# A fused cross-attention kernel: the opening reordered, with the image-prompt V and U products moved into the loop

## The chip, the core and the metric

The kernel runs on one core of one Trainium2 chip. The metric is the time of one execution on the device, in microseconds (us), the median of several runs. Its matmuls are in 32-bit floats, or in pairs of fp32r parts (a high part and the remainder) where precision allows.

## The reference, cut to what matters

Eight batches of 512 tokens (320 channels, 20 heads of 16) attend to 60 text tokens and 4 image-prompt (ip) tokens of a context of width 512.

```python
q = heads(x @ W_q)
k_t, v_t = heads(text @ W_k), heads(text @ W_v)
probs_t  = softmax(q @ k_t.T * D**-0.5)
text_out = probs_t @ v_t
k_ip, v_ip = heads(ip @ W_k_ip), heads(ip @ W_v_ip)
qsem = l2norm(probs_t @ text)
sem  = qsem @ l2norm(ip).T
probs_ip = softmax(q @ k_ip.T * D**-0.5 + 0.5 * sem) * spatial_mask
out = (text_out + probs_ip @ v_ip) @ W_out + b_out + x
```

## The kernel before, in words

The program is written for five engines by hand: each block of the source (`sync`, `gpsimd`, `scalar`, `vector`, `tensor`) is the order of one engine's queue, and semaphores tie them together. Nothing reorders it.

**The loop.** The work is cut into 160 units: 32 tiles of 128 tokens, and 5 groups of 4 heads in each. Twenty units make a batch, ten make a half of 256 tokens. In its slot `u` TensorE (L1230 to L1260) transposes the exps of unit `u + 2`, makes the scores of unit `u + 4`, does at most one task of the table `MISC`, and multiplies unit `u`'s transposed exps with a table (L1062, `table_products`); the table holds the Gram matrix of the context, three differences of ip tokens and V, so that one product gives the weighted sums and what the l2 norm needs. `table_products(u)` waits until ScalarE has copied unit `u - 2` out of the same bank (`copy_fin`). ScalarE's slot `u` (L689) holds in this order: `copy_fin(u - 2)`, a copy of the previous task's bank, the exps of unit `u + 3`, the copy of unit `u + 2`'s transposed exps, and in some slots a few more. VectorE's slot `u` (L886) has the maxima of unit `u + 3`, the end of the previous task, and the quadratic forms of unit `u - 1`.

`MISC` (L278 to L292) gives units their tasks: `q` projects the next half's queries in three parts, `x` transposes the half after that, `at` and `o` (from unit 19 on) transpose a tile's attention and project it to the output. These tasks use the two banks of `mi_ps` in turn, in the order of `MISC_ORDER`; `bank_released` (L311) names the semaphore on which a task waits for its bank, that of two tasks before.

**U.** The ip part of the output is folded into a product: U is W_out applied to the ip differences of V, one row per head and difference. Five U products go to `u_sb`; SP then places batch by batch the rows that belong to it into `u_nat` by small transfers (`place_u`, L355), and once for all batches the last 64 rows of W_out and the bias as broadcasts (`u_shared`, L366, L367). SP waits for all five copies (L364). ScalarE splits a batch's rows into a high part at the end of the slot that `u_batch` names (L716 to L720: unit 12 of each batch) after a wait for `u_shared` and `u_placed`; VectorE makes the low part one slot later (L925).

**The opening** is all that stands before slot 0, and its order is that of the source. SP loads the context in four pairs of batches (the ip tokens once more behind the first pair, L336), x's first half, then W_v, W_k, W_k_ip, W_q (three transfers), W_v_ip, W_out, the mask and more of x. TensorE transposes the context by pairs (L1136), the scaled ip tokens (L1141) and x's first half (L1009, L1011). The transposed context is kept twice: `ctxT`, and `ctxM`, whose ip columns are replaced by differences of the scaled ip tokens (L815 to L820). Gram is `ctxT` times `ctxM` (L1150). ScalarE casts the whole `ctxT` to its high part in one instruction (L653), VectorE subtracts for the low part (L824); the same is done for the weights. V is three products for each pair, high by high, low by high, high by low (L1156): three pairs now, the last one later (L1207). Three K products (L1176) alternate with the first half's three query parts; ScalarE (L667) and VectorE (L843) split K, and POOL (`km_step`, L418) spreads it over heads. Then come the scores of units 0 and 1, the ip V product (`vip`, L1201), V's last pair, x's second half, and, with the scores of units 2 and 3 among them, the five U products (L1216), whose copies ScalarE makes (L682).

Of the kernel before, what the change touches and what calls it, by code (L numbers as in the profile page):

```python
# [35 lines left out]
P = 128  # L36
# [8 lines left out]
def xattn_kernel(nc, x, ctx_tokens, ip_mask, w_q, w_k, w_v, w_k_ip, w_v_ip, w_out, b_out, out):  # L45
# [35 lines left out]
    with es:  # L81
# [17 lines left out]
        def again(place, *shape):  # L99
# [25 lines left out]
        ctxT, ctxM = (  # L125
            place_ctxT[:, EC * B * TOK * n:EC * B * TOK * (n + 1)].rearrange("p (c t) -> p c t", c=EC) for n in range(2))
# [71 lines left out]
        ctxT_act, ctxT_dve, ctxM_text, ctxM_made = (  # L198
            sem("ctxT_act"), sem("ctxT_dve"), sem("ctxM_text"), sem("ctxM_made"))
# [121 lines left out]
        K_BANKS, U_BANKS = (5, 4, 3), (3, 4, 5, 3, 4)  # L321

        def u_batch(u):

            b, s = divmod(u, UNITS)
            return b if s == 12 and b < B else None
# [5 lines left out]
        def _(sp):  # L332
            for q in range(PAIRS):
                sp.dma_start(ctx_nat[:, q, :], ctx_tokens.rearrange("(q b) t e -> q (b t) e", b=2)[q]).then_inc(in_ctx[q], DMA)
                if q == 0:
                    sp.dma_start(ip_nat[:], ctx_tokens[:, T:TOK, :]).then_inc(in_ip, DMA)  # L336
# [3 lines left out]
            sp.dma_start(wkip, w_k_ip.rearrange("(c p) n -> p c n", p=P)).then_inc(in_wkip, DMA)  # L340

# [6 lines left out]
            load_square(wq_nat, w_q, in_wq, (0, 64))  # L348
            sp.dma_start(wvip, w_v_ip.rearrange("(c p) n -> p c n", p=P)).then_inc(in_wvip, DMA)
# [32 lines left out]
        def _(pool):  # L382
# [79 lines left out]
            def builds(t, part):  # L462
# [5 lines left out]
                if k == 0 and b == 0:  # L468
                    pool.wait_ge(v_copied, PAIRS)
# [110 lines left out]
        def _(act):  # L580

            nc.scalar.preload_act_table_set("natural_log_exp_and_others")
# [69 lines left out]
            act.wait_ge(ctxT_dve, 2)  # L652
            nc.scalar.copy(ctx_hi, ctxT).then_inc(ctx_hi_made, 1)  # L653
# [6 lines left out]
            act.wait_ge(in_wo, 2 * DMA)  # L660
            nc.scalar.copy(wo_parts[:, 0], wo[:, 0:2]).then_inc(wo_hi_made, 1)
# [4 lines left out]
            for m in range(QC):  # L666
# [5 lines left out]
                if m > 0:  # L672
                    q_high(0, m - 1)
            q_high(0, 2)
            exps(0)
            exps(1)
            act.wait_ge(pre_v, PAIRS)
# [73 lines left out]
        def _(dve):  # L751
# [55 lines left out]
            for q in (1, 3):  # L807
                dve.wait_ge(pre_ctxT, q + 1)
                v.tensor_copy(ctxT[:, :, P * q:P * q + P], BANKS[q].rearrange("p (c t) -> p c t", c=EC)).then_inc(ctxT_dve, 1)
                if q == 1:  # L810
                    dve.wait_ge(ip_rn_made, 1)
                    v.tensor_scalar(ipn[:], ip_nat[:], ip_rn[:], SEM_SCALE, ALU.mult, ALU.mult).then_inc(ipn_made, 1)

            dve.wait_ge(pre_ipn, 1)
            ip_cols = ctxM.rearrange("p c (b t) -> p (c b) t", t=TOK)  # L815
# [16 lines left out]
            for r in range(2):  # L832
# [3 lines left out]
            by_batch = ctxT.rearrange("p c (b t) -> p c b t", t=TOK)  # L836
            v.tensor_tensor(ip_dif[:, :, :, 0:NDIF], by_batch[:, :, :, T:T + NDIF],
                            by_batch[:, :, :, TOK - 1:TOK].to_broadcast([P, EC, B, NDIF]), ALU.subtract)
            v.tensor_copy(ip_dif[:, :, :, NDIF:NIP], by_batch[:, :, :, TOK - 1:TOK]).then_inc(ip_dif_made, 1)
            dve.wait_ge(wo_hi_made, 1)  # L840
            v.tensor_tensor(wo_parts[:, 1], wo[:, 0:2], wo_parts[:, 0].bitcast(F32), ALU.subtract).then_inc(wo_lo_made, 1)
            for m in range(QC):
# [8 lines left out]
                if m == 1:  # L851
                    q_low(0, 0)
            maxima(0)
            q_low(0, 1)
            maxima(1)
            q_low(0, 2)

            dve.wait_ge(pre_vip, 1)
# [136 lines left out]
        def _(pe):  # L995
# [173 lines left out]
            for q in range(PAIRS - 1):  # L1169
                v_product(q, BANKS[q])  # L1170
# [119 lines left out]
```

## Time and profile before

| | us |
|---|---|
| median of 3 runs (lowest, highest) | 322.41 (321.0, 322.69) |
| the profiled execution | 320.57 |
| its span, first to last instruction | 318.9 |
| start of slot 0 in it | 44.83 |

In that execution PE (TensorE) was busy for 95% of the span, ScalarE (ACT) for 87%, VectorE (DVE) for 84%, GpSimd (POOL) for 66%. The mean granted clock of TensorE was 1.000.

A row of the timeline gives the start, the length, the engine, the line of the source, the operation with its output and inputs, the sizes and how many instructions are merged; in brackets is how long the engine stood idle before and what released it. PEld is TensorE's weight load. Matmuls are pipelined: a merged row ends with the end of its last product, which is later than the start of the next row. A chain of waits is followed back from the last instruction; its pieces are what the end waited for, one after the other.

### The profile page before, as it was taken

Reading aid. Unit: us, or ns where it says so; the run is one execution under the profiler, and the core shown is the slowest. Engines: PE = TensorE matmul, PEld = TensorE weight load, DVE = VectorE, ACT = ScalarE, POOL = GpSimd, SP = SyncE. Lnnn points to the kernel's source line nnn. Section 1 sums busy time; section 2 is a strip of 40 time slices with the busy share of each in tenths; the row PEclk is TensorE's granted clock in tenths of the full one; section 3 lists DMA queues with packets and bytes.
Section 4 is the critical chain, followed back from the end, with each engine's and each line's share of the span. In section 5 each row is a group of like instructions: output and inputs, shape, how many; then the busy total and the mean of one; then the engine's idle time right before and its main releaser. Section 6 shows DMA issues by size and latency. Waiting matters only on the chain.

```text
span 318.9 us, 8813 instructions
## 1 busy us (share of the span) xinstructions
PE 302.9 (95%) x2289; PEld 288.6 (91%) x2289; DVE 268.1 (84%) x1861; ACT 276.3 (87%) x1168; POOL 210.4 (66%) x372
## 2 busy tenths in 40 slices
PE   4899899999999999999999999999999999998976
PEld 3798769888999999999999999999999999998964
DVE  5766847898889888988898889897998899888985
ACT  3736589999999999999999999989999999999942
POOL 3043328688878687878968786778787878676200
PEclk9999999999999999999999999999999999999999
DMA  6980003000120212011201111011202120010011
GB/s 206 346 238 0 1 13 85 2 2 2 32 64 25 62 32 64 24 63 32 63 25 39 47 30 53 15 62 36 62 24 63 34 62 24 23 33 22 23 43 64
DMA packets 15130, 17.02 MB, mean 53 GB/s; under 512 B 2592, under 2 KB 14536, under 8 KB 15080
## 3 DMA queue, kind: packets, MB, share of 16 engines
q1 hardware_dynamic: 15080, 16.44, 16.8%
q8 instruction: 20, 0.33, 0.5%
q14 instruction: 30, 0.25, 0.3%
HBM read 10.55 MB, written 5.24 MB: 50 GB/s over the span
## 4 chain that ended last, share of the span: by engine, by line
PE 70%; DVE 14%; ACT 11%; issue 1%; DMA 1%; POOL 1%; SPq 1%; POOLq 0%
PE gv_ps L1072 19%; PE mi_ps L1107 12%; PE mi_ps L1031 11%; PE et_ps L1059 9%; PE sc_ps L1051 8%; ACT e_sb L619 7%; DVE place_ctxT L795 4%; DVE xl L759 2%; DVE negmax L787 2%; PE mi_ps L1085 2%; PE gv_ps L1186 2%; PE mi_ps L1009 2%; DMA place_ctx<-in_ctx 1%; DVE ktok L847 1%; PE sc_ps L1166 1%
## 5 line engine op out<-in xcount | busy, mean ns | idle before, releaser
L619 ACT ACTIVATE e_sb<-sc_ps,negmax 128x60 f32<-128x60 f32 x640 | 152.0, 349 | 4.9 <-DVE negmax L787 2.9
L795 DVE CUSTOM_DVE_ANT_0 place_ctxT<-gv_ps,e_sb 128x60 f32<-128x60 f32 x640 | 101.0, 213 | 21.9 <-PE gv_ps L1072 19.7
L1072 PE MATMUL gv_ps<-tab,place_w 128*128 128x160 f32 x640 | 113.2, 299 | 0.0
L1072 PEld LDWEIGHTS gv_ps<-tab,place_w 128*128 128x128 f32 x640 | 93.7, 189 | 0.3 <-ACT place_w L637 0.2
L1051 PE MATMUL sc_ps<-km,qs 128*128 128x256 f32 x320 | 77.0, 322 | 0.1
L637 ACT COPY place_w<-et_ps 128x256 f32<-128x256 f32 x160 | 67.0, 419 | 0.2
L1059 PE MATMUL et_ps<-ident,e_sb 128*128 128x128 f32 x320 | 62.6, 277 | 4.4 <-ACT e_sb L619 1.9
L787 DVE TENSOR_REDUCE negmax<-sc_ps 128x4 f32<-128x240 f32 x160 | 63.5, 397 | 0.0
L795 DVE DVE_READ_ACCUMULATOR2_ANT quad<- 128x1 f32 x640 | 52.6, 82 | 0.0
L1059 PEld LDWEIGHTS et_ps<-ident,e_sb 128*128 128x128 f32 x320 | 41.5, 141 | 11.0 <-ACT e_sb L619 9.8
L420 POOL TENSOR_TENSOR km<-ktok,group_mask 128x512 fp32r<-128x512 f32 x40 | 41.3, 1040 | 14.3 <-DVE ktok L847 7.8
L628 ACT COPY fin<-gv_ps 128x80 f32<-128x80 f32 x160 | 43.1, 269 | 6.8 <-DVE quad L795 5.7
L1051 PEld LDWEIGHTS sc_ps<-km,qs 128*128 128x128 f32 x320 | 48.3, 191 | 0.5 <-issue 0.3
L496 POOL TENSOR_TENSOR qs<-q_full,qs 64x256 fp32r<-64x256 f32 x60 | 43.8, 730 | 4.8
L494 POOL CAST qs<-q_full 64x256 fp32r<-64x256 f32 x60 | 23.6, 393 | 27.7 <-ACT q_full L597 25.7
L516 POOL TENSOR_TENSOR mixed<-fin,place_ctxT 128x640 f32<-128x640 f32 (+1 forms) x18 | 21.6, 1202 | 15.7 <-DVE place_ctxT L942 9.7
L786 DVE COPY sip<-sc_ps 128x12 f32<-128x12 f32 x160 | 26.0, 163 | 3.3 <-PE sc_ps L1051 3.1
L1107 PE MATMUL mi_ps<-wo_parts,attnT 128*128 128x320 f32 x120 | 22.8, 311 | 0.0
L884 DVE TENSOR_TENSOR place_w<-mi_ps,x_nat 128x320 f32<-128x320 f32 x31 | 14.9, 484 | 5.3 <-PE mi_ps L1107 5.3
L433 POOL COPY tab<-g_sb 60x315 f32<-60x315 f32 x32 | 14.8, 461 | 6.5 <-POOL tab L433 3.1
L1107 PE MATMUL mi_ps<-wo_parts,attnT_low 128*128 128x320 f32 x60 | 19.0, 323 | 0.0
L1031 PE MATMUL mi_ps<-xl,wq_hi 128*128 128x256 f32 (+1 forms) x96 | 19.0, 279 | 0.0
(184 smaller groups left out, 550.6 us busy)
## 6 DMA issues: line engine op xcount, KB each, us to landing
x_nat<-in_x SPq DMA_DIRECT2D x16, 320.0 KB, 3.1
out<-place_w SPq DMA_DIRECT2D x32, 160.0 KB, 1.8
place_ctx<-in_ctx SPq DMA_DIRECT2D x4, 256.0 KB, 3.1
place_w<-in_L_xattn_W_v SPq DMA_DIRECT2D x1, 640.0 KB, 6.3
place_w<-in_L_xattn_W_k SPq DMA_DIRECT2D x1, 640.0 KB, 7.6
place_w<-in_L_xattn_W_k_ip SPq DMA_DIRECT2D x1, 640.0 KB, 9.0
place_w<-in_L_xattn_W_v_ip SPq DMA_DIRECT2D x1, 640.0 KB, 9.1
place_ctxT<-in_L_xattn_W_out SPq DMA_DIRECT2D x1, 640.0 KB
```

What stands on the lines that cost most here:

```text
L420: g.tensor_tensor(km[:, b % 2, c].rearrange("p s (j t) -> p s j t", t=TOK), ktok[:, :, c, TOK * b:TOK * b + TOK].unsqueeze(2).to_broadcast ...
L496: g.tensor_tensor(qs[other, half % 2, c, :], q_full[own, m, :], qs[own, half % 2, c, :].bitcast(F32), ALU.subtract).then_inc(q_part, 1)
L619: last = nc.scalar.activation(e_sb[:, slot, TOK * j:TOK * j + T], sc_ps[:, bank, TOK * j:TOK * j + T], ACT.Exp, bias=negmax[:, slot, j:j + 1])
L628: nc.scalar.copy(fin[:, t % TILES, GROUP * c:GROUP * c + GROUP, :], ps[:, :, T:TABW]).then_inc(fin_copied, 1)
L637: nc.scalar.copy(eT[:, u % TRING, :], et_ps[:, u % 2, 0:2 * P]).then_inc(eT_copied, 1)
L787: v.tensor_reduce(negmax[:, u % ERING, :], ps[:, :, 0:T], AX_X, ALU.max, negate=True).then_inc(max_done, 1)
L795: last = v.tensor_tensor_reduce(out=junk[:, u % 2, j, 0:T], in0=gv_ps[:, u % 2, TABW * j:TABW * j + T], in1=e_sb[:, u % ERING, TOK * j:TOK ...
L1031: last = mm(to, w, xx, start=n == 0, stop=n == len(steps) - 1)
L1051: last = mm(sc_ps[:, u % 2, 0:GROUP * TOK], q, km[:, parity, c, part, :], start=part == 0, stop=part == 1)
L1059: last = tr(et_ps[:, u % 2, P * r:P * r + P], e_sb[:, u % ERING, P * r:P * r + P], ident[:])
L1072: last = mm(gv_ps[:, u % 2, 2 * TABW * r:2 * TABW * r + 2 * TABW], eT[:, u % TRING, P * r:P * r + P], tab[:, b % 2, h:h + 2, :].rearrange( ...
L1107: last = mm(ps, steps[n][0], steps[n][1], start=n == 0, stop=n == len(steps) - 1)
```

## The change

- **One context copy.** `ctxM` is gone. VectorE makes all four copies of `ctxT` and the ip differences (now right behind them), and then the ip columns of `ctxT` itself are overwritten; Gram is `ctxT` times `ctxT`.
- **The high part by quarters.** ScalarE casts each pair from the transposes' bank, behind VectorE's copy.
- **Idle products.** TensorE does 9 transposes of the identity, whose result nobody reads, before the first context pair, and 3, 2, 2 and 1 behind the pairs.
- **V by parts.** High by high for three pairs, then low by high, then high by low.
- **The order behind.** The scores of units 0 and 1 come before the third K product; on ScalarE the exps of units 0 and 1 come before the third K copies, on VectorE the maxima before the third K low parts. The casts of W_out move behind the first query copies.
- **Loads.** The ip tokens are loaded from ScalarE's queue, W_k_ip comes behind W_q.
- **Tasks.** `vip` becomes the task of unit 1, the U products those of units 4, 6, 9, 11 and 12. VectorE makes their copies, one slot later, behind the quadratic forms. Batch 0's split of U moves from unit 12 to unit 16.

```diff
+        VIP_AT, U_AT, U0_AT = 1, (4, 6, 9, 11, 12), 16
+        MISC[VIP_AT] = ("vip", 0, 0)
+        for n, at in enumerate(U_AT):
+            MISC[at] = ("u", n, 0)
...
+                    "vip": (vip_made, QC), "u": (u_copied, n + 1),
...
         def u_batch(u):
 
+            if u == U0_AT:
+                return 0
             b, s = divmod(u, UNITS)
-            return b if s == 12 and b < B else None
+            return b if s == 12 and 0 < b < B else None
...
         def _(sp):
             for q in range(PAIRS):
                 sp.dma_start(ctx_nat[:, q, :], ctx_tokens.rearrange("(q b) t e -> q (b t) e", b=2)[q]).then_inc(in_ctx[q], DMA)
-                if q == 0:
-                    sp.dma_start(ip_nat[:], ctx_tokens[:, T:TOK, :]).then_inc(in_ip, DMA)
...
-            sp.dma_start(wkip, w_k_ip.rearrange("(c p) n -> p c n", p=P)).then_inc(in_wkip, DMA)
...
             load_square(wq_nat, w_q, in_wq, (0, 64))
+            sp.dma_start(wkip, w_k_ip.rearrange("(c p) n -> p c n", p=P)).then_inc(in_wkip, DMA)
...
         def _(act):
 
+            act.dma_start(ip_nat[:], ctx_tokens[:, T:TOK, :]).then_inc(in_ip, DMA)
             nc.scalar.preload_act_table_set("natural_log_exp_and_others")
...
             for q in range(PAIRS):
-                if q % 2 == 0:
-                    act.wait_ge(pre_ctxT, q + 1)
-                    nc.scalar.copy(ctxT[:, :, P * q:P * q + P],
-                                   BANKS[q].rearrange("p (c t) -> p c t", c=EC)).then_inc(ctxT_act, 1)
-                else:
-                    act.wait_ge(ctxT_dve, q // 2 + 1)
-                nc.scalar.copy(ctxM[:, :, P * q:P * q + P].rearrange("p c (b t) -> p c b t", t=TOK)[:, :, :, 0:T],
-                               BANKS[q].rearrange("p (c b t) -> p c b t", b=2, t=TOK)[:, :, :, 0:T]).then_inc(ctxM_text, 1)
+                act.wait_ge(ctxT_made, q + 1)
+                nc.scalar.copy(ctx_hi[:, :, P * q:P * q + P],
+                               BANKS[q].rearrange("p (c t) -> p c t", c=EC)).then_inc(ctx_hi_made, 1)
             x_hi(0, 0)
             x_hi(0, 1)
-            act.wait_ge(ctxT_act, 2)
-            act.wait_ge(ctxT_dve, 2)
-            nc.scalar.copy(ctx_hi, ctxT).then_inc(ctx_hi_made, 1)
...
+            k_high(0)
+            q_high(0, 0)
+            act.wait_ge(in_wo, 2 * DMA)
+            nc.scalar.copy(wo_parts[:, 0], wo[:, 0:2]).then_inc(wo_hi_made, 1)
+            k_high(1)
+            q_high(0, 1)
             exps(0)
             exps(1)
+            k_high(2)
+            q_high(0, 2)
             act.wait_ge(pre_v, PAIRS)
...
             copy_eT(0)
-            for n in range(5):
-                rows = 96 + B * (n % 2 == 0)
-                act.wait_ge(pre_u, n + 1)
-                nc.scalar.copy(u_sb[0:rows, n], BANKS[U_BANKS[n]][0:rows, 0:C]).then_inc(u_copied, 1)
             exps(2)
             copy_eT(1)
...
-            for q in (1, 3):
+            for q in range(PAIRS):
                 dve.wait_ge(pre_ctxT, q + 1)
-                v.tensor_copy(ctxT[:, :, P * q:P * q + P], BANKS[q].rearrange("p (c t) -> p c t", c=EC)).then_inc(ctxT_dve, 1)
+                v.tensor_copy(ctxT[:, :, P * q:P * q + P], BANKS[q].rearrange("p (c t) -> p c t", c=EC)).then_inc(ctxT_made, 1)
...
+            by_batch = ctxT.rearrange("p c (b t) -> p c b t", t=TOK)
+            dve.wait_ge(ctxT_made, PAIRS)
+            v.tensor_tensor(ip_dif[:, :, :, 0:NDIF], by_batch[:, :, :, T:T + NDIF],
+                            by_batch[:, :, :, TOK - 1:TOK].to_broadcast([P, EC, B, NDIF]), ALU.subtract).then_inc(ip_dif_made, 1)
...
+            def copy_u(n):
+
+                rows = 96 + B * (n % 2 == 0)
+                dve.wait_ge(pre_u, n + 1)
+                v.tensor_copy(u_sb[0:rows, n], mi_ps[0:rows, misc_bank(("u", n, 0)), 0:C]).then_inc(u_copied, 1)
+
+            k_low(0)
+            q_low(0, 0)
+            dve.wait_ge(wo_hi_made, 1)
+            v.tensor_tensor(wo_parts[:, 1], wo[:, 0:2], wo_parts[:, 0].bitcast(F32), ALU.subtract).then_inc(wo_lo_made, 1)
+            k_low(1)
+            q_low(0, 1)
             maxima(0)
-            q_low(0, 1)
             maxima(1)
+            k_low(2)
             q_low(0, 2)
...
+                if kind == "vip":
+                    spread_vip()
+                if kind == "u":
+                    copy_u(m)
...
+            def idle_products(n):
+
+                for _ in range(n):
+                    tr(BANKS[4][:, 0:P], ident[:], ident[:])
+
             pe.wait_ge(ident_made, 1)
+            idle_products(9)
             for q in range(PAIRS):
...
                 last.then_inc(pre_ctxT, 1)
+                idle_products((3, 2, 2, 1)[q])
...
+            for part in range(3):
+                if part == 1:
+                    pe.wait_ge(ctx_lo_made, 1)
+                if part == 2:
+                    pe.wait_ge(wv_lo_made, 1)
+                for q in range(PAIRS - 1):
+                    v_steps(q, BANKS[q], part)
...
+            k_product(0)
+            pe.wait_ge(wq_lo_made, 1)
+            q_project(0, 0)
+            pe.wait_ge(g_copied, 2)
+            k_product(1)
+            q_project(0, 1)
+            pe.wait_ge(v_copied, 2)
             scores(0)
             scores(1)
+            k_product(2)
+            pe.wait_ge(wq_pair_made, 2)
+            q_project(0, 2)
             pe.wait_ge(q_lo, 2)
-            v_product(PAIRS - 1, mi_ps[:, 1, :])
+            for part in range(3):
+                v_steps(PAIRS - 1, mi_ps[:, 1, :], part)
             x_transposes(1, 0)
             x_transposes(1, 1)
             pe.wait_ge(zeros_made, 6)
+            pe.wait_ge(v_copied, 3)
             e_transposes(0)
+            scores(2)
             pe.wait_ge(k_lo, 2 * GROUPS)
...
             e_transposes(1)
             scores(3)
...
+                if kind == "vip":
+                    vip_product()
+                if kind == "u":
+                    u_product(n)
```

`vip_product` and `u_product` hold the matmuls of L1201 to L1205 and L1222, each behind a wait for its bank of `mi_ps`; the first U product also waits for the spread ip V (`vip_made`).

## Rows read from the trace of the kernel before

**Rows 1.** Windows by stage: us, then busy us (instructions) of each engine, clock, DMA.

```profile
44.83:59.40 14.57, 14.01 (x107) 13.07 (x107) 10.75 (x93) 14.05 (x64) 10.36 (x15) 1.00 0.24 54
59.40:74.85 15.45, 14.76 (x110) 13.43 (x111) 13.46 (x112) 15.10 (x70) 10.96 (x21) 1.00 0.00 1
74.85:92.02 17.17, 16.92 (x131) 16.47 (x131) 14.69 (x115) 15.97 (x71) 15.12 (x25) 1.00 0.14 42
```

**Rows 2.** The chain of waits, 26 to 45 us: start, us, what.

```profile
34.98 2.29 PE gv_ps L1203 x24
...
42.25 0.54 PE et_ps L1222 x2
...
43.96 0.82 ACT e_sb L619 x4
```

**Rows 3.** Timeline of TensorE in the opening.

```profile
3.42 1.09 PE L1136 MATMUL sc_ps<-ident,place_ctx 128*128 128x128 f32 x4 [3.42 <-DMA place_ctx<-in_ctx]
...
8.74 0.65 PE L1009 MATMUL mi_ps<-ident,x_nat 128*128 128x128 f32 x4
...
9.58 3.84 PE L1150 MATMUL gv_ps<-place_ctxT 128*128 128x128 f32 x32
...
18.03 0.75 PE L1166 MATMUL sc_ps<-u_all,km 128*128 128x320 f32 x4
...
20.39 1.99 PE L1186 MATMUL gv_ps<-km,u_all 128*128 128x480 f32 x8
...
24.92 1.92 PE L1186 MATMUL gv_ps<-km,u_all 128*128 128x480 f32 x8
...
28.36 0.60 PE L1031 MATMUL mi_ps<-xh,wq_hi 128*128 128x256 f32 x3
```

**Rows 4.** Timeline of VectorE in the opening.

```profile
5.30 0.14 DVE L806 TENSOR_SCALAR ip_ssc<-ip_ss 32x1 f32<-32x1 f32 x1
...
8.42 0.69 DVE L809 COPY place_ctxT<-et_ps 128x512 f32<-128x512 f32 x1 [0.95 <-PE et_ps L1136]
...
12.42 2.29 DVE L824 TENSOR_TENSOR ctx_lo<-place_ctxT,km 128x2048 fp32r<-128x2048 f32 x1 [1.04 <-ACT km L653]
...
29.80 2.85 DVE L847 SCALAR_TENSOR_TENSOR ktok<-gv_ps,ktok 64x512 fp32r<-64x512 f32 x4 [1.61 <-ACT ktok L670]
32.68 0.86 DVE L771 TENSOR_TENSOR qs<-mi_ps,qs 64x256 fp32r<-64x256 f32 x2
```

**Rows 5.** Timeline of ScalarE in the opening.

```profile
28.56 2.44 ACT L670 ACTIVATE ktok<-gv_ps 64x512 fp32r<-64x512 f32 x4 [2.02 <-PE gv_ps L1188]
31.02 0.75 ACT L611 CAST qs<-mi_ps 64x256 fp32r<-64x256 f32 x2
```

**Rows 6.** Timeline of SP, its DMA issues.

```profile
1.25 0.89 SPq L336 DMA_DIRECT2D ip_nat<-in_ctx  x1
...
43.99 1.64 SPq L359 DMA_DIRECT2D place_ctxT<-place_w  x2
...
49.05 0.69 SPq L367 DMA_DIRECT2D place_ctxT<-in_L_xattn_b_out  x1
```

**Rows 7.** The chain of waits, 83 to 89 us: one set of tasks.

```profile
83.12 0.33 PE mi_ps L1085 x3
...
86.03 0.73 PE mi_ps L1107 x5
...
88.20 0.59 PE mi_ps L1107 x4
```

**Rows 8.** Windows of one us; the last two columns are DMA share and GB/s.

```profile
52.00:53.00 1.00, 1.00 (x11) 1.00 (x10) 1.00 (x11) 0.95 (x6) 0.86 (x3) 1.00 0.69 126
```

**Rows 9.** Timeline of all engines, 64 to 71 us.

```profile
65.02 0.91 DVE L928 TENSOR_TENSOR u_all<-place_ctxT,u_all 128x320 fp32r<-128x320 f32 x1
...
70.02 0.43 ACT L637 COPY place_w<-et_ps 128x256 f32<-128x256 f32 x1
```

**Rows 10.** Timeline of TensorE near the end.

```profile
310.24 0.52 PE L1085 MATMUL mi_ps<-ident,mixed 128*128 128x128 f32 x3 [2.18 <-DVE mixed L966]
```

More of the change, by code:

```diff
@@ L664, in _, with k_high @@
                 nc.scalar.copy(v_sb[:, q, :], BANKS[q][:, 0:C]).then_inc(v_copied, 1)
-            for m in range(QC):
+            def k_high(m):
                 act.wait_ge(pre_k, m + 1)
@@ L835, in _, with k_low @@
                               ).then_inc(g_copied, 1)
[L836 to L842, printed above, removed]
+            def k_low(m):
                 for a in range(QROWS[m] // 64):
@@ L1152, in _, with v_steps @@
             last.then_inc(pre_g, 1)
+            pe.wait_ge(ctx_hi_made, PAIRS)
             pe.wait_ge(wv_hi_made, 1)
-            def v_product(q, bank):
+            def v_steps(q, bank, part):
                 tokens = slice(P * q, P * q + P)
-                steps = [(cc[:, c, tokens], ww[:, c, :]) for cc, ww in ((ctx_hi, wv_hi), (ctx_lo, wv_hi), (ctx_hi, wv_lo))
-                         for c in range(EC)]
-                for n, (cc, ww) in enumerate(steps):
-                    if q == 0 and n == EC:
-                        pe.wait_ge(ctx_lo_made, 1)
-                    if q == 0 and n == 2 * EC:
-                        pe.wait_ge(wv_lo_made, 1)
-                    last = mm(bank[:, 0:C], cc, ww, start=n == 0, stop=n == len(steps) - 1)
-                last.then_inc(pre_v, 1)
@@ L1169, in _ @@
[L1169 to L1180 removed]
+                cc, ww = ((ctx_hi, wv_hi), (ctx_lo, wv_hi), (ctx_hi, wv_lo))[part]
@@ new lines, in v_steps @@
+                for c in range(EC):
+                    last = mm(bank[:, 0:C], cc[:, c, tokens], ww[:, c, :], start=part == c == 0, stop=part == 2 and c == EC - 1)
+                if part == 2:
+                    last.then_inc(pre_v, 1)
+            for part in range(3):
+                if part == 1:
+                    pe.wait_ge(ctx_lo_made, 1)
+                if part == 2:
+                    pe.wait_ge(wv_lo_made, 1)
+                for q in range(PAIRS - 1):
+                    v_steps(q, BANKS[q], part)
@@ L1190, in _, with vip_product @@
                 last.then_inc(pre_k, 1)
-                if m == 0:
-                    pe.wait_ge(wq_lo_made, 1)
-                if m == QC - 1:
-                    pe.wait_ge(wq_pair_made, 2)
-                q_project(0, m)
+            def vip_product():
+                pe.wait_ge(in_wvip, DMA)
+                pe.wait_ge(*bank_released(("vip", 0, 0)))
+                bank = mi_ps[:, misc_bank(("vip", 0, 0)), :]
+                for m in range(QC):
+                    for c in range(EC):
+                        last = mm(bank[0:QROWS[m], 32 * m:32 * m + 32].rearrange("p (b n) -> p b n", n=NIP),
+                                  wvip[:, c, P * m:P * m + QROWS[m]], ip_dif[:, c], start=c == 0, stop=c == EC - 1)
+                last.then_inc(pre_vip, 1)
@@ new lines, in u_product @@
+            def u_product(n):
+                m, part = (n // 2, n % 2) if n < 4 else (2, 0)
+                if n == 0:
+                    pe.wait_ge(vip_made, QC)
+                    pe.wait_ge(in_wo, 2 * DMA)
+                pe.wait_ge(*bank_released(("u", n, 0)))
+                rows = 96 + B * (part == 0)
+                first = 0 if part == 0 else 96 + B
+                mm(mi_ps[0:rows, misc_bank(("u", n, 0)), 0:C], vip_bd[0:QROWS[m], m, first:first + rows], wo[0:QROWS[m], m, :],
+                   start=True, stop=True).then_inc(pre_u, 1)
@@ L1196, in _ @@
+            pe.wait_ge(wk_lo_made, 1)
+            pe.wait_ge(ip_dif_made, 2)
+            pe.wait_ge(in_wkip, DMA)
+            k_product(0)
[5 more added lines that the diff above has]
+            pe.wait_ge(v_copied, 2)
             scores(0)
             scores(1)
-            pe.wait_ge(in_wvip, DMA)
-            pe.wait_ge(k_lo, 4)
-            for m in range(QC):
-                for c in range(EC):
-                    last = mm(BANKS[5][0:QROWS[m], 32 * m:32 * m + 32].rearrange("p (b n) -> p b n", n=NIP),
-                              wvip[:, c, P * m:P * m + QROWS[m]], ip_dif[:, c], start=c == 0, stop=c == EC - 1)
```

77 lines of the change are left out of this document (26 added, 51 removed).

## The prediction

> **What bounds the kernel now.** I read the windows first, cut at the starts of units 0, 10, 20 and 30 of the loop [rows 1]. From unit 20 on TensorE sets the pace: 16.92 of 17.17 us busy. In units 0 to 9 ScalarE is as full (14.05 of 14.57), and these ten units are 2.6 us shorter, because no attention transposes and output products run yet: TensorE has room there, but little. All that stands before 44.83 is the opening, a chain through three engines. The chain of waits there [rows 2] shows what the change moves: the image-prompt V product (vip) costs TensorE 2.29 us, one U product 0.54 (five of them), and the exps at 43.96 end at 44.79, on which unit 0 starts. The timelines give the steps of the opening: TensorE's [rows 3], VectorE's [rows 4], ScalarE's [rows 5]; SP's issues are in [rows 6].
>
> **The opening until Gram.** The first four context transposes last 1.09 us, four of the same size from 8.74 only 0.65 [rows 3]: the profile's granted clock is 1.00 throughout [rows 1], its level of 2.4 GHz, yet the early ones run at half of that (0.22 us each), and nothing but transposes came before the speed doubled. The change puts 17 idle transposes between them, and the context loads no longer stand behind the image-prompt load (0.89 us of SP, [rows 6]), which goes to ScalarE's queue, ahead of ScalarE's first copy. So pairs 1 to 3 land some 0.9 us sooner. VectorE now makes all four copies: free at about 5.15 (its scale steps end 5.44 now, [rows 4], and come up to 0.3 sooner with the load), it needs 4 x 0.65 for the copies and some 1.55 for four short steps between and behind them (estimates of 0.3 to 0.5 from the 0.69 of the widest copy, [rows 4]): 9.3. Gram starts at about 9.45 instead of 9.58 [rows 3]: nearly nothing won. This takes the speed to double near 5.2 us, after about as much unbroken transposing as before. Had it stayed low, 9 + 16 + 8 transposes at 0.22 from 1.55 would end at 8.85, and Gram would start near 10.8.
>
> The Trainium skill ("TensorE: Matmul & The Clock Gate", Part 4) says that transposes do not count as busy work for the clock; by that the idle transposes would only delay, and the sum would be 1.35 us worse. The trace of before disagrees: only transposes preceded the doubling.
>
> **From Gram to unit 0.** Gram stays 3.84 us [rows 3] and ends 13.3. The high part by quarters lets VectorE start the low part (2.29, [rows 4]) at 10.6 instead of 12.42; it ends at 12.9. V's 36 matmuls then run without a gap, nine groups of four at 0.59 (four of them from 18.03 to 20.39, [rows 3]), and end at 18.55 where 20.39 stood. K's first product and the first query part take 4.53, the second K product 3.44 [rows 3]: 26.5, before 28.36. From here the path is ScalarE and VectorE in turn: four high copies 2.44 and two query copies 0.75 [rows 5] to 29.9; VectorE's four low parts (2.85) end near 30.85, the query lows take 0.86 more [rows 4], two maxima about 0.5 each: 32.7. The second exps (0.82 for four, [rows 2]) end at 34.0, and only then come the last K high copies, which the new order puts behind the exps: 35.2; their low parts 36.65, the last query part's 37.5. TensorE, done with V's last product at 33.8, waits for that bank until 37.5. Then x transposes, x copies, x lows, maxima and the exps of unit 2 follow in turn, 3.75 in all: 41.25. vip and U are gone from the path. **Unit 0 starts at 41.3, 3.5 us sooner** (2.2 if the clock stays low; 4.0 if the hand-overs are tighter). Moving W_k_ip behind W_q's three loads in SP's queue is costed at nothing: V covers it until 18.5; each us that it lands later is a us lost. W_q, V's and W_out's loads all come sooner or keep their place.
>
> **The moved tasks in the loop.** Unit 1 gets vip, units 4, 6, 9, 11, 12 a U product each. A steady half of ten units takes 17.17 [rows 1] with two sets of attention transposes and two output products, 2 x (0.33 + 0.73 + 0.59) = 3.30 [rows 7]. Units 0 to 9 get 2.29 + 3 x 0.54 = 3.91 in their place: 17.8 at TensorE's pace throughout; counted unit by unit from the end of vip, with its waits, 17.3. Against 14.57 that is +2.9 (ends: +1 if waits hide more, +3.2). The two U products in units 11 and 12 add 1.08, less about 0.3 that TensorE idles there (14.76 of 15.45 busy): +0.8. So unit 13 stands at -3.5 + 2.9 + 0.8 = +0.2. VectorE's part (six short vip copies, five U copies of 320 columns, by the 512-column copy of 0.69 some 0.43 each) lies beside TensorE's; VectorE has room, 10.75 of 14.57 busy. Were it full, each U copy would cost its 0.43.
>
> **The wait this creates.** SP places batch 0's U rows and the shared rows only when the last U copy is done. Before, that was at 43.96 [rows 2]; eight issues ran from 43.99 to 49.74 [rows 6], and the 640 KB of the broadcast moved until about 52.7 (the DMA share is 0.69 from 52 to 53, [rows 8]). So 8.8 us pass from the last U copy to the landing. Before, units 0 to 12 hid them. Now U's last copy is made in VectorE's unit 13, where the low part of those rows stood (65.02, [rows 9]): with +0.2 for the unit, -0.3 for a VectorE less crowded there and 0.43 for the copy it ends at 65.35. The landing is at 74.15. ScalarE comes to the split, now in unit 16 behind the copy of unit 18 (70.02, done 70.28, [rows 9]), no later than 70.3, and stands there for some 4 us. Queued behind it are the table copy of unit 15, the exps of unit 20 and the copy of unit 19; TensorE waits for the first of them at the table product of unit 17, VectorE for both. ScalarE sets units 17 to 19 as before, so nothing is won back; behind unit 20 TensorE is full. The sum: 74.15 - 70.28 + 0.3 for the split itself = **+4.2 us**. Its ends: each us at unit 13 is a us here; the eight issues alone take 5.75 [rows 6] and the data must follow, so the landing can't come under 7 us: +2.4; +6 with the low clock and more waits in the loop.
>
> The profiled execution took 320.57 for a span of 318.9; the median of the runs is 322.41, 0.6% higher. With +4.2 the first becomes 324.8, the median 326.6; I give the latter. A measurement of this kernel tells about 0.5%, 1.6 us, from no change.
>
> **Rivals.**
> 1. *The clock falls in the new idle stretches.* TensorE would idle 3.7 us before unit 0 and over 4 in unit 17. The trace has an idle of 2.18 us, and the three transposes behind it take 0.52 [rows 10], full speed (at 0.22 apart they would take over 0.8); only the start is longer idle, and there the speed was half, from 3.42 until before 8.74. Half speed for 5 us costs up to 2.5 each time, partly under the other engines: +2.5 in all, 329.1. The Trainium skill ("TensorE: Matmul & The Clock Gate", the part on HAM oscillation) says that an idle gap between bursts can send the clock back to half; no run here shows it yet.
> 2. *The idle transposes only delay*: +1.35, 328.0.
> 3. *The loop hides the moved products*: vip and U cost units 0 to 12 about 1 us instead of 3.7. U's last copy and the landing come 2.7 us sooner: +1.5, 323.9. For it: ScalarE bounds units 0 to 9. Against it: TensorE's room there is 0.56 us of 14.57.
> 4. *ScalarE doesn't stand at the split* (the other side). Its place is unit 16, its price the whole wait; it decides where the landing comes within 4.7 us of the last U copy. Then the loop's units 13 to 19 run at TensorE's pace, up to 15.45 - (17.17 - 3.30) = 1.6 less, and unit 20 stands at +0.2 - 1.5 = -1.3: 321.1, down to 319.4 if the loop hides more. For it: the landing has no row, I read it from the DMA share. Against it: SP's issues alone take 5.75.
>
> **How the numbers follow.** Forecast 0.52; rival 1 0.13, rival 2 0.12, rival 3 0.10, rival 4 0.13. The range leaves out most of rival 4 and the top of rival 1: 322.2 (an early landing and a loop that hides its products) to 329.4 (half speed in one of the stretches). Faster by over 0.5% is the better half of rival 4, 0.07; within 0.5% the rest of it and half of rival 3, 0.12; slower 0.81.
>
> **What would show it.** Unit 0's first transposes near 41.3 with exps before them; Gram near 9.45 and the first K product near 18.5; a wait of TensorE of 3 to 4 us before the x transposes of half 1; units 0 to 9 at 17 to 18 us; the first split on ScalarE behind an idle time of about 4 us that the W_out broadcast ends, and TensorE's table product of unit 17 idle behind it. Wrong it is if ScalarE has no such idle time, or if U's last copy is done before 63.

## The result and the profile after

The changed kernel takes 330.32 us (median of four runs, 327.77 to 331.42); the kernel before, run beside it, 322.55. The ratio is 1.0237, its 95% interval 1.0201 to 1.0273. The forecast was 326.6 with 329.4 as the upper end: the sign and the place of the loss are right, the size is not. The profiled execution, the shortest of the four, took 327.77 us for a span of 326.0.

First the windows of the changed kernel, cut at the end of V, the first instruction behind it, and the starts of units 0, 10, 13, 17 and 20 (columns as in [rows 1]):

```profile
33.90:37.60 3.70, 0.00 (x0) 0.00 (x0) 2.21 (x4) 1.90 (x5) 0.88 (x1) 0.94 0.00 0
37.60:42.04 4.44, 3.14 (x14) 2.96 (x14) 2.00 (x6) 2.29 (x8) 1.33 (x4) 0.67 0.01 2
42.04:59.76 17.72, 17.67 (x137) 16.55 (x138) 12.07 (x99) 14.38 (x64) 10.37 (x15) 1.00 0.01 2
59.76:65.21 5.45, 5.45 (x38) 4.67 (x38) 5.11 (x41) 4.64 (x22) 2.83 (x5) 1.00 0.01 5
65.21:71.32 6.11, 5.90 (x47) 5.50 (x46) 4.98 (x45) 5.67 (x27) 4.78 (x10) 1.00 0.06 13
71.32:82.42 11.10, 6.39 (x34) 6.11 (x34) 4.44 (x34) 5.15 (x22) 4.28 (x10) 0.69 0.27 62
82.42:99.13 16.71, 16.58 (x134) 16.34 (x132) 14.57 (x113) 15.62 (x71) 14.10 (x22) 1.00 0.12 36
```

The same boundaries in the trace of before (units 0 to 9 are in [rows 1]; here follow units 10 to 12, 13 to 16 in two pieces, and 17 to 19) give the whole account:

```profile
59.40:63.64 4.24, 4.24 (x33) 3.93 (x33) 3.52 (x30) 4.07 (x20) 1.79 (x4) 1.00 0.00 0
63.64:68.97 5.33, 4.93 (x38) 4.62 (x38) 4.89 (x43) 5.21 (x26) 4.41 (x8) 1.00 0.01 2
68.97:70.23 1.26, 1.16 (x10) 0.92 (x8) 1.22 (x12) 1.26 (x8) 1.12 (x2) 1.00 0.00 0
70.23:74.85 4.62, 4.43 (x33) 3.95 (x34) 3.83 (x31) 4.57 (x21) 3.64 (x8) 1.00 0.01 2
```

| stretch | before | after | difference |
|---|---|---|---|
| start of unit 0 | 44.83 | 42.04 | -2.79 |
| units 0 to 9 | 14.57 | 17.72 | +3.15 |
| units 10 to 12 | 4.24 | 5.45 | +1.21 |
| units 13 to 16 | 6.59 | 6.11 | -0.48 |
| units 17 to 19 | 4.62 | 11.10 | +6.48 |
| start of unit 20 | 74.85 | 82.42 | +7.57 |

Behind unit 20 the two are alike: 243.6 us to the end after, 244.1 before. The reader is to see that units 17 to 19 make the result, and that TensorE was busy for 6.39 of 11.10 us there, at a mean granted clock of 0.69.

What stood still there, first the timeline of ScalarE, then that of TensorE (both of the changed kernel):

```profile
71.08 0.45 ACT L643 COPY place_w<-et_ps 128x256 f32<-128x256 f32 x1
76.42 0.46 ACT L719 CAST u_all<-place_ctxT 128x320 fp32r<-128x320 f32 x1 [4.89 <-DMA place_ctxT<-in_L_xattn_b_out]
```

```profile
37.63 1.09 PE L1029 MATMUL mi_ps<-ident,x_nat 128*128 128x128 f32 x4 [3.74 <-DVE qs L777]
...
71.84 0.60 PE L1029 MATMUL mi_ps<-ident,x_nat 128*128 128x128 f32 x4
77.15 1.40 PE L1092 MATMUL gv_ps<-tab,place_w 128*128 128x160 f32 x4 [4.71 <-ACT fin L634]
...
82.42 0.38 PE L1079 MATMUL et_ps<-ident,e_sb 128*128 128x128 f32 x2
```

L719 is the split of batch 0's rows: ScalarE stands 4.89 us there, by the profile for the bias broadcast (issued last, behind the 640 KB of W_out's rows and on the same semaphore), and TensorE 4.71 us behind it, at unit 17's table product, as the forecast named them. The other idle stretch of TensorE, 3.74 us ahead of x's second half, is there too. Behind either of them the same work takes twice as long: four x transposes 1.09 us at 37.63 and 0.60 at 71.84, a table product 1.40 at 77.15 where others take 0.71.

The chain of waits of the changed kernel (start, us, what) tells why the landing is where it is:

```profile
66.06 0.41 DVE place_w L873
...
66.49 0.90 SPq L362
67.44 0.79 SPq L362
68.27 0.71 SPq L363
69.02 0.57 SPq L365
69.64 0.59 SPq L365
70.27 0.58 SPq L365
70.89 0.70 SPq L369
71.64 4.76 DMA place_ctxT<-in_L_xattn_b_out
76.42 0.46 ACT u_all L719
```

Last U copy (done 66.47), eight issues in a row on SP, landing: 9.95 us. The eighth issue, 0.69 us from 71.64, lies inside the DMA piece.

### The profile page after: what moved, and what is told of

Read it like the earlier page. It is cut to its first block, busy times and chain, and to the rows that moved or that the text cites. A ratio compares the mean times of both kernels' runs of the same rounds, so it can differ in the third digit from the quotient of the medians.

```text
span 326.0 us, 8847 instructions
## 1 busy us (share of the span) xinstructions
PE 306.2 (94%) x2306; PEld 294.9 (90%) x2306; DVE 270.1 (83%) x1868; ACT 272.2 (83%) x1160; POOL 209.8 (64%) x372
## 4 chain that ended last, share of the span: by engine, by line
PE 73%; DVE 15%; ACT 6%; SPq 1%; DMA 1%; issue 1%; POOL 1%; POOLq 0%; DVEq 0%
PE gv_ps L1092 21%; PE mi_ps L1127 12%; PE mi_ps L1051 10%; PE et_ps L1079 9%; PE sc_ps L1071 9%; ACT e_sb L625 5%; DVE place_ctxT L794 4%; DVE xl L758 2%; DVE ktok L850 2%; PE mi_ps L1029 2%; DVE negmax L786 2%; PE mi_ps L1105 2%; DMA place_ctxT<-in_L_xattn_b_out 1%; PE gv_ps L1176 1%; PE sc_ps L1188 1%
## 5 line engine op out<-in xcount | busy, mean ns | idle before, releaser
L1092 PE MATMUL gv_ps<-tab,place_w 128*128 128x160 f32 x640 | 114.6, 302 | 4.8 <-ACT fin L634 4.7
L1092 PEld LDWEIGHTS gv_ps<-tab,place_w 128*128 128x128 f32 x640 | 95.0, 191 | 6.6 <-issue 5.1
L1071 PE MATMUL sc_ps<-km,qs 128*128 128x256 f32 x320 | 77.9, 325 | 0.0
L423 POOL TENSOR_TENSOR km<-ktok,group_mask 128x512 fp32r<-128x512 f32 x40 | 41.3, 1040 | 20.3 <-DVE ktok L850 11.2
L1079 PEld LDWEIGHTS et_ps<-ident,e_sb 128*128 128x128 f32 x320 | 42.8, 143 | 8.7 <-ACT e_sb L625 8.5
L1071 PEld LDWEIGHTS sc_ps<-km,qs 128*128 128x128 f32 x320 | 49.2, 195 | 0.0
L634 ACT COPY fin<-gv_ps 128x80 f32<-128x80 f32 x160 | 42.4, 265 | 7.3 <-DVE quad L794 6.1
```

The lines of the kernel that those rows point to most:

```text
L423: g.tensor_tensor(km[:, b % 2, c].rearrange("p s (j t) -> p s j t", t=TOK), ktok[:, :, c, TOK * b:TOK * b + TOK].unsqueeze(2).to_broadcast ...
L634: nc.scalar.copy(fin[:, t % TILES, GROUP * c:GROUP * c + GROUP, :], ps[:, :, T:TABW]).then_inc(fin_copied, 1)
L1071: last = mm(sc_ps[:, u % 2, 0:GROUP * TOK], q, km[:, parity, c, part, :], start=part == 0, stop=part == 1)
L1079: last = tr(et_ps[:, u % 2, P * r:P * r + P], e_sb[:, u % ERING, P * r:P * r + P], ident[:])
L1092: last = mm(gv_ps[:, u % 2, 2 * TABW * r:2 * TABW * r + 2 * TABW], eT[:, u % TRING, P * r:P * r + P], tab[:, b % 2, h:h + 2, :].rearrange( ...
```

## The experiments

Theory A: the loss is the wait at the split, made by the late U copies; the low clock behind the idle stretches is an addition. The rivals: the moved products, the idle transposes, or the order of the opening cost it.

### The wait

**e1_split20**: the split of batch 0 comes four units later.

```diff
-        VIP_AT, U_AT, U0_AT = 1, (4, 6, 9, 11, 12), 16
+        VIP_AT, U_AT, U0_AT = 1, (4, 6, 9, 11, 12), 20
```

> Only the split of batch 0's U rows moves, from unit 16 to unit 20. Theory A (the loss is ScalarE's wait for the landing, and the half clock behind it): the landing stays near 76.4, ScalarE comes to the split near 75.5, so its idle time falls from 4.9 to 1 us or less, the clock stays at 1.00 from unit 1 on, unit 20 starts near 75.5 to 76.5 instead of 82.4, ratio to the kernel before 1.002 to 1.006. Theory B (the loss is the moved vip and U products, which overfill the loop): the wait only stood where TensorE would have been late anyway; ratio stays at 1.015 or more.

Measured: 321.61 us (321.45 to 325.05, ten runs), ratio 1.0002 (0.9970 to 1.0035). The timeline of ScalarE of this kernel has the split with no idle time ahead of it, and the windows of units 0 and 1 show what its profiled execution lost instead:

```profile
79.05 0.52 ACT L719 CAST u_all<-place_ctxT 128x320 fp32r<-128x320 f32 x1
```

```profile
41.47:45.16 3.69, 3.69 (x17) 3.65 (x18) 0.48 (x2) 2.11 (x10) 0.39 (x1) 0.50 0.02 7
45.16:48.92 3.76, 3.76 (x33) 3.68 (x32) 1.14 (x10) 1.77 (x8) 2.88 (x4) 0.92 0.01 2
```

One constant takes away 8.7 us of the median (330.32 - 321.61), and by the ratios to before (1.0237 and 1.0002) all of the loss. Unit 0 took 3.69 us at clock 0.50 here, 2.00 at 1.00 in the changed kernel's profile (42.04 to 44.04): how long the clock stays low behind the first idle stretch differs by execution. Six of the ten runs, with a mean clock of 0.995, took 321.45 to 321.70; the four below 0.99 took 322.77 to 325.05. The profiled one is among the four; its unit 20 starts at 77.33, later than the 76.5 expected.

**e2_shared_early**: the two broadcasts don't need U; SP issues them behind x's loads, after waits for what the region they overwrite still holds.

```diff
+            sp.wait_ge(pre_g, 1)
+            sp.wait_ge(ip_dif_made, 2)
+            sp.wait_ge(ctx_lo_made, 1)
+            sp.dma_start(u_nat[0:64], w_out[2 * P:C, :] ...).then_inc(u_shared, DMA)
+            sp.dma_start(u_nat[127:128], b_out ...).then_inc(u_shared, DMA)
             sp.wait_ge(u_copied, 5)
             place_u(0)
-            sp.dma_start(u_nat[0:64], w_out[2 * P:C, :] ...).then_inc(u_shared, DMA)
-            sp.dma_start(u_nat[127:128], b_out ...).then_inc(u_shared, DMA)
```

> SP issues the two broadcasts before it waits for the U copies; the split stays in unit 16. Theory A with the broadcasts as the late part: from the last U copy to the split there are six issues (4.3 us) and some 2 us to land, 6.3 instead of 9.9; ScalarE's idle time at the split falls from 4.9 to about 1.3, the clock doesn't fall there, ratio 1.007 to 1.011. If the placed rows are the late part (the six small transfers, not the broadcast), the idle time stays over 4 and the ratio near 1.024.

Measured: 323.96 us (322.34 to 324.48, ten runs), ratio 1.0055 (1.0033 to 1.0077). The timeline of ScalarE of this kernel:

```profile
72.07 0.46 ACT L722 CAST u_all<-place_ctxT 128x320 fp32r<-128x320 f32 x1 [0.33 <-DMA place_ctxT<-place_w]
```

The last U copy ends at 66.68, six issues follow, and the rows have landed at 71.99, 5.3 us later. With the split still in unit 16 the wait is 0.33 us. Two kernels with nothing else in common lose the wait, the first with all of the loss, the second with about three quarters of it (2.37% down to 0.55%): theory A. The rest in the second goes with the clock: its two runs with a mean clock of 0.995, the profiled one among them, took 322.34 and 322.36, the eight at 0.984 or 0.989 took 323.84 to 324.48.

### The clock

Three kernels fill the idle stretches with transposes that nobody reads; the wait at the split stays.

**e3_warm_gap** fills the first one.

```diff
             for part in range(3):
                 v_steps(PAIRS - 1, mi_ps[:, 1, :], part)
+            pe.wait_ge(k_lo, 8)
+            idle_products(28)
```

> 28 idle transposes fill TensorE's idle stretch before the x transposes of half 1. Theory A: the granted clock stays 1.00 from 34 to 42, the six x transposes take 1.0 instead of 1.7, unit 0 starts near 41.3 instead of 42.04; all else stays: 0.7 us, ratio 1.019 to 1.024. If the clock falls for another reason than the idle stretch, it is at 0.5 from 38 to 40 as before, and the ratio is the same.

Measured: 329.71 us (327.91 to 330.01, four runs), ratio 1.0236 (1.0194 to 1.0279). Its TensorE timeline:

```profile
34.19 3.22 PE L1155 MATMUL gv_ps<-ident 128*128 128x128 f32 x28
38.08 0.63 PE L1029 MATMUL mi_ps<-ident,x_nat 128*128 128x128 f32 x4 [0.67 <-DVE qs L777]
...
42.04 0.44 PE L1079 MATMUL et_ps<-ident,e_sb 128*128 128x128 f32 x2 [2.19 <-ACT e_sb L625]
```

The x transposes run at full speed (0.63), and from their start to unit 0 it is 3.96 us, where the changed kernel took 4.41: TensorE waits for most of what it wins, 2.19 us at the exps. So the low clock costs 0.45 us of the opening; it costs more where it reaches into the loop. In this execution V ended 0.4 later, and unit 0 starts at 42.04 again.

**e5_warm_stall** fills the second one: 42 transposes in unit 17 ahead of the table product, into the bank of an x task.

```diff
+                if u == U0_AT + 1:
+                    pe.wait_ge(*bank_released(("x", 1, 3)))
+                    for _ in range(42):
+                        tr(mi_ps[:, misc_bank(("x", 1, 3)), 0:P], ident[:], ident[:])
                 if not early and u < ALL_UNITS:
                     table_products(u)
```

> 42 idle transposes stand ahead of the table product of unit 17, so TensorE works while ScalarE waits at the split. Theory A: the wait stays 4.9 us, but the clock stays 1.00 from 72 to 82; unit 17's table product takes 0.7 instead of 1.40 and unit 20 starts 1.1 us sooner, near 81.3; where executions differ by how long the clock stays low, the spread of the runs narrows; ratio 1.014 to 1.021. If the half clock costs nothing (ScalarE sets the pace behind the wait): the same 1.024.

Measured: 330.0 us (329.92 to 330.69, four runs), ratio 1.0262 (1.0227 to 1.0296). The TensorE timeline, and the windows of unit 0 and of the stall:

```profile
73.95 4.75 PE L1302 MATMUL mi_ps<-ident 128*128 128x128 f32 x42
79.22 0.78 PE L1092 MATMUL gv_ps<-tab,place_w 128*128 128x160 f32 x4 [0.52 <-ACT fin L634]
...
83.36 0.44 PE L1079 MATMUL et_ps<-ident,e_sb 128*128 128x128 f32 x2 [0.17 <-ACT e_sb L625]
```

```profile
42.20:45.72 3.52, 3.50 (x16) 3.50 (x17) 0.49 (x2) 1.95 (x9) 0.21 (x1) 0.53 0.02 7
72.00:84.00 12.00, 10.88 (x86) 9.77 (x86) 6.05 (x48) 6.66 (x29) 5.82 (x13) 1.00 0.25 58
```

The clock holds in the stall, and from the split (78.49) to unit 20 it is 4.9 us instead of 6.0: the low clock costs 1.1 us there. But unit 0 ran at 0.53 in this execution and lost 1.5, and the ratio lies above the 1.014 to 1.021 of theory A: in the median nothing is won.

**e12_warm_both** has both edits.

> The idle transposes of e3_warm_gap and those of e5_warm_stall together, so that both idle stretches of TensorE are filled with work that nobody reads; the wait at the split stays. Theory A (of the loss, the wait, the moved products and the late landing take some 6.5 us whatever the clock does; the half clock behind the two stretches takes the rest, 1 to 3 us, and scatters the runs): mean clock 0.995 or higher, unit 20 at 81 to 82 us, time 327.5 to 329, the runs within 1 us of each other. Theory B (the clock matters little, the time goes to the wait alone): 330 to 331 as in the changed kernel.

Measured: 329.07 us (328.08 to 330.18, four runs; 328.3 profiled, clock 0.995), ratio 1.0220 (1.0180 to 1.0260). Unit 20 starts at 81.79, as theory A has it, though one issue of SP took 1.13 us instead of 0.59 and the landing came at 76.93. The median lies 1.25 us under the changed kernel's, but just above theory A's range; the runs lie 2.1 us apart and not within 1, and the intervals of the ratios overlap. So the clock's share of the median is not settled closer than between nothing and some 2.5 us, an estimate from these intervals. What is settled: with the clock up in both stretches 7 us of the loss remain.

**e4_no_idle** takes the 17 idle transposes of the start out.

```diff
-            idle_products(9)
...
-                idle_products((3, 2, 2, 1)[q])
```

> The 17 idle transposes of the start are taken out, nothing else. Theory A (transposes count as work for the clock; the idle ones bring the doubling forward from about 8.3 to about 6.0 us): the speed doubles near 8 us or later again, Gram (L1176's line) starts 0.5 to 1.5 us later than 9.5, V ends later by the same, and the kernel is 0 to 1 us slower than the changed kernel, the wait at the split being what it was. Theory B (transposes count for nothing, the idle ones only delay, rival 2 of the prediction): Gram starts about 1.3 us sooner, and the kernel is about 1.3 us faster than the changed kernel.

Measured: 330.28 us (328.85 to 331.16, four runs), ratio 1.0256 (1.0226 to 1.0286). In its profile x's transposes still take 1.12 us for four at 8.89, and Gram is later and longer (9.49 and 3.84 us with the idle ones); unit 0 starts at 43.69.

```profile
10.22 5.20 PE L1174 MATMUL gv_ps<-place_ctxT 128*128 128x128 f32 x32
```

Theory B would have Gram sooner, and falls; but at the scatter of this kernel the median shows no difference. The same question was put again without the wait, in e9 below.

### The opening

**e6_order** undoes the new order of the third K copies.

```diff
-            exps(0)
-            exps(1)
             k_high(2)
             q_high(0, 2)
+            exps(0)
+            exps(1)
...
-            maxima(0)
-            maxima(1)
             k_low(2)
             q_low(0, 2)
+            maxima(0)
+            maxima(1)
```

> In the opening the third K copies and the last query part's copies come before the first exps on ScalarE, and their low parts before the first maxima on VectorE; the split stays in unit 16. Theory A (the new order is what makes TensorE idle 3.7 us ahead of x's second half, and the low clock follows from the idleness): x transposes start at 34 to 35 us instead of 37.6, without an idle gap over 1.5 us, the clock stays at 1.00 there, unit 0 starts near 40 to 41, the wait at the split stays 4.5 to 5 us, and the kernel is 1 to 3 us faster than the changed one: 327.5 to 329. Theory B (the gap is only moved, since maxima and exps must be made in any case): unit 0 near 42, no gain over 0.5 us.

Measured: 329.52 us (327.75 to 330.03, four runs), ratio 1.0227 (1.0194 to 1.0260). Its TensorE timeline:

```profile
35.48 0.63 PE L1029 MATMUL mi_ps<-ident,x_nat 128*128 128x128 f32 x4 [1.02 <-DVE qs L777]
37.97 0.44 PE L1031 MATMUL mi_ps<-ident,x_nat 128*128 128x128 f32 x2 [1.87 <-ACT place_ctx L681]
...
41.11 0.69 PE L1079 MATMUL et_ps<-ident,e_sb 128*128 128x128 f32 x2 [1.11 <-ACT e_sb L625]
```

The gap of 3.74 us became two of 1.02 and 1.87, and one of 1.11 ahead of unit 0 stayed; unit 0 starts 0.9 us sooner, but the clock fell all the same, behind the second gap and ahead of the third (0.57 from 37.97 to 41.11), and unit 0 took 3.69 us at 0.50. A miss of theory A: most of the idle time is only moved, since the maxima and exps have to be made in any case.

**e10_order_split20** is this order with the split of e1_split20.

> The order of e6_order and the split of e1_split20 together. Theory A (two separate losses: the wait at the split, and the gap of the opening with the low clock behind it): 318.5 to 320.5, 1 to 3 us under e1_split20's 321.6, ratio to before 0.989 to 0.995. Theory B (with the wait gone the loop behind sets the pace and the opening's gain is swallowed): 321 to 322, ratio 0.997 to 1.0.

Measured: 321.98 us (321.09 to 323.90, ten runs), ratio 1.0008 (0.9987 to 1.0028), no better than e1_split20, with a mean clock of 0.984 or 0.989 in every run. Again theory A misses.

**e7_u_in_opening** puts vip and U back into the opening, but into the idle places that the new order has made: vip ahead of the third K product, three U products where TensorE waited 3.74 us, two around the scores of unit 2. The split is in unit 12 again, and the loop has no new task.

```diff
             scores(1)
+            vip_product()
             k_product(2)
...
+            for n in range(3):
+                u_product(n)
             x_transposes(1, 0)
             x_transposes(1, 1)
...
             e_transposes(0)
+            u_product(3)
             scores(2)
+            u_product(4)
```

> vip and the five U products go back into the opening, but into TensorE's idle places of the new order (vip ahead of the third K product, U products 0 to 2 ahead of x's second half, 3 and 4 around the scores of unit 2); ScalarE makes their copies; the split is in unit 12 again. The rest of the change stays. Theory A (the opening's reordering gains, the moved tasks lose): unit 0 at 41 to 43 us, units 0 to 12 at the pace of before (19 us), no idle time at the split, unit 20 at 72 to 73.5, time 319 to 321, ratio 0.988 to 0.997. Theory B (the opening gained only because vip and U left it): unit 0 at 44.5 or later, ratio 1.0 or more.

Measured: **317.9 us** (317.28 to 319.04, four runs), ratio 0.9880 (0.9856 to 0.9904). Run again as e13_u_opening_again:

> The kernel of e7_u_in_opening once more, to stand beside the next one on the same chip: 317.5 to 318.5, ratio 0.986 to 0.990.

317.94 us (317.62 to 319.18, six runs), ratio 0.9877 (0.9848 to 0.9906). It beats both kernels. Windows of e7_u_in_opening (the stretch from V's last product to unit 0, units 0 to 9, 10 to 12, 13 to 19):

```profile
33.84:42.11 8.27, 7.43 (x44) 5.53 (x42) 4.40 (x11) 6.72 (x20) 2.21 (x4) 1.00 0.00 1
42.11:56.67 14.56, 13.99 (x107) 13.04 (x107) 10.37 (x91) 13.96 (x64) 10.37 (x15) 1.00 0.23 53
56.67:60.91 4.24, 4.24 (x32) 3.94 (x33) 3.51 (x30) 4.07 (x20) 1.79 (x4) 1.00 0.00 0
60.91:72.15 11.24, 10.55 (x79) 9.49 (x79) 9.95 (x84) 11.08 (x51) 9.20 (x18) 1.00 0.01 3
```

Unit 0 starts at 42.11, 0.07 later than with vip and U in the loop: in the idle places six products cost nothing. Behind it the loop runs as before (14.57 and 4.24 in the account above). Filled, the stretch keeps the clock at 1.00. So the rewritten opening wins 2.7 us in the profile (44.83 to 42.11), 4 in the median, and moving the products into the loop lost all of it and more.

**e9_u_opening_no_idle** is e7_u_in_opening without the idle transposes.

> e7_u_in_opening without the 17 idle transposes of the start. Theory A (they bring the full clock forward): Gram 0.4 to 2 us later, and since nothing behind waits for a transfer, unit 0 and the whole kernel later by the same: 318.3 to 320, ratio 0.989 to 0.995. Theory B (the transposes count for nothing, or the opening behind Gram has slack for them): 317.5 to 318.3, or faster.

Measured: 320.1 us (318.25 to 321.91, twelve runs), ratio 0.9930 (0.9902 to 0.9958). Its TensorE timeline, in an execution that was among the shorter ones (318.62):

```profile
8.85 1.11 PE L1020 MATMUL mi_ps<-ident,x_nat 128*128 128x128 f32 x4
...
10.19 4.04 PE L1165 MATMUL gv_ps<-place_ctxT 128*128 128x128 f32 x32
```

With idle transposes x's four take 0.66 at about the same time, and Gram starts 0.2 to 0.4 sooner and takes 3.84. The idle transposes are worth 2.2 us of the median here, about half of what this opening wins: theory A, just above its range. Not all of that is the later Gram: six of the twelve runs have a mean clock of 1.00 and took 318.25 to 319.85, about 0.9 more than the five such runs with the idle ones (317.62 to 318.04), and the other six, at 0.995, took 320.35 to 321.91. In this profile unit 0 starts at 42.70, 0.4 to 0.6 later than with them; what the longer of the twelve runs lose beyond that has no trace, and stays open.

**e14_one_cast** is e7_u_in_opening with the context's high part in one cast again.

```diff
-            for q in range(PAIRS):
-                act.wait_ge(ctxT_made, q + 1)
-                nc.scalar.copy(ctx_hi[:, :, P * q:P * q + P], BANKS[q] ...).then_inc(ctx_hi_made, 1)
             x_hi(0, 0)
             x_hi(0, 1)
+            act.wait_ge(ip_cols_made, 1)
+            nc.scalar.copy(ctx_hi, ctxT).then_inc(ctx_hi_made, 1)
```

> e7_u_in_opening with the high part of the context cast in one instruction again, as before the change, behind x's copies; V stays in parts. Theory A (V by parts is what lets the low part lie beside the first twelve V matmuls; the quarters are worth nothing of their own): the cast ends near 12.3 us, the low part near 14.6, both ahead of the V part that reads them (about 13.5 and 15.4), V ends near 18.9 as with quarters, time within 0.5 us of 317.9. Theory B (the quarters are what closes V's gaps): V ends 1 to 2 us later, time 319 to 320.

Measured: 318.25 us (317.47 to 319.66, six runs), ratio 0.9880 (0.9842 to 0.9919). The cast runs from 10.79 to 12.69, the low part from 12.71 to 15.00, and V's second part starts at 15.83 with no idle time. The median is 0.3 us above e7_u_in_opening's, within the scatter of either, so the runs show no worth of the quarters. That V by parts closes the gaps, because the low part then lies beside Gram and V's first part, is read from this trace; no kernel here takes the parts back.

## Why the prediction was right about the place of the loss and wrong about its size

**The opening until the last query part came true to 0.15 us.** Gram at 9.49 (forecast 9.45), V done at 18.45 (18.55), and the idle time of TensorE from 33.9 to 37.63 (33.8 to 37.5). One step of it was wrong without harm: the speed was to double near 5.2 us and did so near 6.3, but Gram waited for VectorE (0.58 us idle ahead of it), not for the transposes. The last piece, 3.75 us, took 4.41: unit 0 at 42.04 instead of 41.3. Of the 0.66 more, 0.45 is the low clock and 0.2 the hand-overs (3.96 in e3_warm_gap).

**The loop hid nothing**: +3.15 and +1.21, together 4.36 where the sum had 3.7. The working had found 17.8 at TensorE's pace and taken less for waits that might overlap; it is 17.72, and 5.45 of 5.45 us in units 10 to 12. Rival 3 falls.

**The wait is where and what it was forecast to be**; rival 4, no wait, falls. The step that failed is the size of "The wait this creates": three terms of its sum came out too small, each by 1.1 to 1.2 us, and only the three together lead out of the range. The first is "So 8.8 us pass from the last U copy to the landing." It is 9.95. The issues take about what they took before (5.84 us against 5.75). The forecast read the landing from the DMA share in windows of one us [rows 8], as 52.7. In windows of 0.2 us the bytes of before still move until about 53.2, 9.2 us behind the last U copy, and in the changed kernel until about 75.6, 9.1 us behind it. ScalarE starts almost a us after that. The first line is of the kernel before, the others of the changed one:

```profile
53.00:53.20 0.20, 0.20 (x4) 0.20 (x3) 0.20 (x1) 0.20 (x3) 0.20 (x1) 1.00 0.03 6
...
75.40:75.60 0.20, 0.00 (x0) 0.00 (x0) 0.00 (x0) 0.00 (x0) 0.20 (x1) 0.50 0.11 19
75.60:75.80 0.20, 0.00 (x0) 0.00 (x0) 0.00 (x0) 0.00 (x0) 0.20 (x1) 0.50 0.00 0
```

The last bytes move before 75.60, and the wait ends at 76.40: 0.8 us in which nothing moves. The Trainium skill ("DMA: Bandwidth & Descriptors", Anatomy of one DMA) says of transfers issued by GpSimd that the semaphore is only set once the last byte is confirmed in the target memory. SP issues these; the trace fits the rule, with its 0.8 us, but doesn't show what fills them.

The other two terms: the last U copy ended at 66.47 instead of 65.35 (+1.12: unit 0 and the loop, less what was gained behind), and the landing came 1.15 us later behind it than the forecast had it. From the split to unit 20, 6.0 us passed instead of 4.87 (+1.13): the sum had put the clock at nothing there, and with the clock up it is 4.87 (e5_warm_stall). With the 4.2 of the sum that is 7.6, and 7.57 was measured.

**Rival 1, the low clock, came true beside the forecast**, in both stretches; its chance of 0.13 was too low, because [rows 10] (2.18 us idle, full speed behind) was taken to speak for 3.7 and 4.7 us too. Its price, forecast as 2.5 us in all, is 1.1 us in the stall; in the first stretch 0.45 in the changed kernel's profile, and 1.5 to 1.7 more in unit 0 of other kernels' profiles. Where the changed kernel's other three runs (mean clock 0.969 to 0.979, the profiled one 0.984) lost their further 1.7 to 3.7 us, no trace of theirs shows: a slow unit 0 would cover the shortest of them, not the longest.

**Rival 2, that the idle transposes only delay, falls.** In the changed kernel only transposes stood before the doubling, which came near 6.3 us:

```profile
5.05 1.06 PE L1162 MATMUL sc_ps<-ident,place_ctx 128*128 128x128 f32 x4
...
6.33 0.65 PE L1162 MATMUL et_ps<-ident,place_ctx 128*128 128x128 f32 x4
```

That is sooner than in the kernels without the idle ones (before: behind 8 us; e4_no_idle: behind 10). In e12_warm_both transposes alone held the clock at 1.00 through both stretches. The Trainium skill ("TensorE: Matmul & The Clock Gate", Part 4) says that transposes don't count as busy work for the clock in the way that matmuls do. For the transposes of this kernel, in 32-bit floats, the runs disagree: Gram starts at 9.49 with the idle ones and at 10.22 without.

## What to carry to other kernels

Work taken off the path of an opening has consumers: follow each of its results to the first instruction that waits for it, and count its whole chain (here eight issues, the data, and 0.8 us behind the last bytes: 10 us from the end of the copy) before choosing where it goes. Look for idle places of the engine on the path before moving work into a loop where that engine is full; there it also kept the clock up (1.00 in e7_u_in_opening). If a transfer doesn't need the late result, issue it ahead of the wait.

## What was not expected of the hardware

- Behind an idle stretch of 3.7 us the half clock lasted until before unit 0 in one execution (42.04) and through unit 0 in others (to 45.2 in e1_split20, 47.3 in e4_no_idle). Behind two gaps of 1.0 and 1.9 us, with four transposes between, it fell as well (e6_order).
- At the start the granted clock reads 1.00 all along in the changed kernel too (0 to 10 us), while four transposes follow each other in 0.86 us (3.56 to 4.42) and later in 0.49 (6.33 to 6.82): there only the durations show the low level.
